# First pair's up products placed beside the last two sequences, and key products of a batch in two row groups

## What is computed

```python
x = x + L0_attn(layernorm(x))   # gated delta rule, 8 key heads, 16 value heads, head size 64
x = x + L0_ffn(layernorm(x))    # 8 routed experts (top 2) and a shared one, hidden size 176
x = x + L1_attn(layernorm(x))   # softmax attention, 16 heads of 8, and a gelu MLP
x = x + L1_ffn(layernorm(x))    # 8 routed experts (top 2) and a shared one, hidden size 512
```

```python
S = S * exp(g_t)                          # g_t: log decay of a value head
delta = (v_t - S.T @ k_t) * b_t
S = S + outer(k_t, delta);  o_t = S.T @ q_t
```

## Time and profile before

| what | value |
|---|---|
| median of 3 runs | 1583.46 us (1576.72 to 1585.36) |
| the profiled execution, its own time | 1569.76 us |
| its span, first to last instruction | 1567.9 us |
| mean TensorE clock granted in it | 0.878 of full speed |
| PE busy | 1321.6 us, 84% of the span |
| DVE busy | 911.5 us |
| ACT busy | 726.7 us |

### The profile page before, as it was taken

The page is one execution under the profiler, slowest core; times in us unless marked ns, Lnnn a source line. Parts: engine busy times, 40 slices in busy tenths (PEclk is TensorE's granted clock), DMA queues, the critical chain, the costliest instruction groups (busy, mean ns, idle before and its releaser), DMA issues.

```text
span 1567.9 us, 26862 instructions
## 1 busy us (share of the span) xinstructions
PE 1321.6 (84%) x11048; PEld 956.3 (61%) x11048; DVE 911.5 (58%) x2365; ACT 726.7 (46%) x1353; POOL 194.2 (12%) x186
## 2 busy tenths in 40 slices
PE   2759889798979979887859786989899988989899
PEld 2345767566666756656846453676566655676567
DVE  4696878979697897968134623463344524354321
ACT  1547465664746566472414143523444344533442
POOL 5011121212122121212020001000000001000000
PEclk9768869798896978887679777999999999999999
DMA  3000000000000000000210000000000000000000
GB/s 120 4 1 4 1 2 11 2 11 2 11 1 2 11 2 8 2 30 2 84 75 1 8 1 0 0 8 1 1 8 1 8 1 7 1 1 1 2 7 8
DMA packets 15066, 17.69 MB, mean 11 GB/s; under 512 B 2567, under 2 KB 13216, under 8 KB 14560
## 3 DMA queue, kind: packets, MB, share of 16 engines
q1 hardware_dynamic: 12768, 14.09, 2.7%
q0 software_dynamic: 576, 1.76, 0.3%
q10 hardware_dynamic: 1600, 0.12, 0.1%
HBM read 13.87 MB, written 2.10 MB: 10 GB/s over the span
## 4 chain that ended last, share of the span: by engine, by line
PE 60%; DVE 25%; ACT 9%; issue 3%; POOL 1%; DMA 1%; SPq 0%; DVEq 0%; ACTq 0%
PE ps L1405 8%; PE ps L1395 8%; PE ps L1354 6%; PE ps L1036 5%; DVE arena L1746 4%; DVE arena L1749 4%; PE ps L1018 4%; DVE arena L1990 2%; ACT arena L900 2%; PE ps L1497 2%; PE ps L1094 2%; PE ps L1461 2%; PE ps L1074 2%; PE ps L1003 1%; PE ps L1184 1%
## 5 line engine op out<-in xcount | busy, mean ns | idle before, releaser
L1664 DVE SCALAR_TENSOR_TENSOR arena<-ps,conv_w,arena 128x255 f32<-128x255 f32 (+2 forms) x384 | 163.8, 475 | 19.4 <-ACT arena L609 14.9
L853 ACT ACTIVATE arena<-ps 128x512 f32<-128x512 f32 x144 | 85.2, 597 | 180.7 <-PE ps L1395 180.6
L1405 PEld LDWEIGHTS ps<-arena 128*128 128x128 f32 x1152 | 132.6, 192 | 24.8 <-issue 9.9
L1405 PE MATMUL ps<-arena 128*128 128x128 f32 x1152 | 136.9, 277 | 7.1 <-ACT arena L853 4.1
L1395 PE MATMUL ps<-arena 128*128 128x512 f32 x288 | 134.3, 612 | 0.0
L516 POOL TENSOR_TENSOR rstd<-var_eps,half_power 128x2 f32<-128x2 f32 (+1 forms) x28 | 23.3, 832 | 650.9 <-DVE var_eps L1635 650.9
L1911 DVE SCALAR_TENSOR_TENSOR arena<-ps,gates,arena 128x128 f32<-128x128 f32 x128 | 36.0, 343 | 114.0 <-PE ps L1405 113.7
L1036 PE MATMUL ps<-arena 64*128 64x256 f32 x256 | 82.9, 462 | 16.1 <-ACT arena L618 16.1
L1732 DVE TENSOR_TENSOR arena<-ps,arena 128x512 f32<-128x512 f32 x64 | 44.1, 689 | 81.9 <-PE ps L1036 70.5
L2027 DVE TENSOR_REDUCE arena<-ps 128x8 f32<-128x2048 f32 (+1 forms) x24 | 54.9, 2292 | 62.2 <-PE ps L1461 62.2
L1036 PEld LDWEIGHTS ps<-arena 64*128 64x128 f32 x256 | 52.4, 220 | 62.0 <-DVE arena L1734 24.1
(11 more groups left out here) (246 smaller groups left out, 2904.0 us busy)
## 6 DMA issues: line engine op xcount, KB each, us to landing
arena<-in_routed_up SPq DMA_DIRECT2D x1, 2048.0 KB, 9.6
arena<-in_routed_down SPq DMA_DIRECT2D x1, 2048.0 KB, 15.0
x_ln<-in_x SPq DMA_DIRECT2D x8, 128.0 KB, 2.2
arena<-in_w_mix SPq DMA_DIRECT2D x1, 1024.0 KB, 11.0
x_in<-in_x SPq DMA_DIRECT2D x8, 128.0 KB, 2.4
out_x<-x_res SPq DMA_DIRECT2D x8, 128.0 KB, 1.9
arena<-out_x SPq DMA_DIRECT2D x4, 256.0 KB, 2.7
out_x<-arena SPq DMA_DIRECT2D x4, 256.0 KB, 2.2
```

The source lines that it names most:

```text
L853: act.activation(hid1[half][:, i, :], ps[:, banks[i], :], ACT.Gelu).then_inc(s["mgelu"], 1)
L1405: mm = pe.matmul(ps[:, bank, c * P:(c + 1) * P], hid1[half][:, i, c * P:(c + 1) * P], m_down[:, e, i, :], start=(i == 0), stop=(i == HT1 - 1))
L1664: ins = dve.scalar_tensor_tensor(conv_tile(f, m)[:, sh:SEQ], ps[:, PAIR_BANK[p], j * SEQ:(j + 1) * SEQ - sh], conv_w[:, m, TAPS - 1 - sh:T ...
```

## The change

1. **Key products.** Batch b of a chunk takes heads b and b + 4, on partitions 0 to 63 and 64 to 127, and each writes to a bank of its own (3 and 4 for even batches, 5 and 6 for odd ones). The 16 value heads of a batch's sums, exponentials and products are picked to match (`batch_of`, `batch_rows`). The other users of the banks move: the small results from bank 3 to bank 2, tokens of v from 3 and 4 to 2 and 4, transposed heads of the second chunk from 5 and 6 to 7 and 2. Waits change with them: the first key products wait for all 8 convolutions (for 3 before), `solve` of the first chunk waits for all products of the next sequence, and stands behind `project(f, 0)`.
2. **The first pair.** The first pair is loaded, normed and transposed in iteration 6. Its up tiles 0 to 4 stand in iteration 6, tiles 5 to 12 and the routing in iteration 7, tile 13 behind the last projection, each on PE, ACT and DVE. For this pair two sets of two banks are used (three before) and one product buffer; there are 3 gate buffers (4 before). Later pairs keep the order of before.

```diff
@@ -72,15 +72,22 @@
-PAIR_BANK = (0, 1, 2, 4, 3, 4, 3, 4)
-KK_BANK = (2, 4)
+PAIR_BANK = (0, 1, 3, 4, 2, 4, 2, 4)
+KK_BANKS = ((3, 4), (5, 6))
+HT_BANKS = ((6, 6), (7, 2))
+V_BANKS = (2, 4)
+FIRST_TURN, FIRST_LOGITS = (0, 7), (2, 6)
...
@@ -387,6 +409,11 @@
+                if it == SEQS - 2:
+                    sp.wait_ge(s["o_psum"], 4 * (SEQS - 1))
+                    sp.wait_ge(s["x1_stored"], 16 * 2)
+                    sp.dma_start(pair_in[:, :, :], pair(out, 0)).then_inc(s["pair_loaded"], 16)
                 if has_i:
                     sp.wait_ge(s["x_updated"], CH * (it + 1))
...
-            sp.dma_start(pair_in[:, :, :], pair(out, 0)).then_inc(s["pair_loaded"], 16)
...
+            def gate_of_tile(p, k):
+                act.wait_ge(s["up_psum"], p * UP0 + k + 1)
+                act.activation(gate3[k % 3], ps[:, up_bank(p, k) + 1, :], ACT.Identity, bias=b3[:, UP_ORDER[k]:UP_ORDER[k] + 1])\
+                    .then_inc(s["gate_done"], 1)
...
                 if has_i:
                     squares(i, 0)
+                if it == SEQS - 1:
+                    hidden_tiles_of(0, 5)
+                    gate_of_tile(0, 6)
+                    gate_of_tile(0, 7)
+                    router(0, 0)
+                if has_i:
                     solutions(i, 1)
+                if it == SEQS - 1:
+                    hidden_tiles_of(0, 7)
...
@@ -1024,17 +1100,17 @@
                 if k == 0:
                     pe.wait_ge(s["qk_silu"], QK_TILES * (n + 1))
-                    pe.wait_ge(s["conv_done"], NP * n + 3)
+                    pe.wait_ge(s["conv_done"], NP * (n + 1))
                 elif k == 1:
-                    pe.wait_ge(s["conv_done"], NP * (n + 1))
+                    after(pe, "u64_ready", 4 * n)
...
-                    m, r = khead(2 * b + g)
-                    mm = pe.matmul(ps[:, KK_BANK[k % 2], 2 * P * g:2 * P * (g + 1)].rearrange("p (q n) -> p q n", q=2),
-                                   mix_qk[n % 2][r:r + DH, QK_TILES + m, cs], mix_qk[n % 2][r:r + DH, m::QK_TILES, cs],
+                    r = DH * g
+                    mm = pe.matmul(ps[:, KK_BANKS[k % 2][g], 0:2 * P].rearrange("p (q n) -> p q n", q=2),
+                                   mix_qk[n % 2][r:r + DH, QK_TILES + b, cs], mix_qk[n % 2][r:r + DH, b::QK_TILES, cs],
                                    start=True, stop=True)
...
@@ -1136,9 +1212,8 @@
                     pe.wait_ge(s["u64_ready"], 4 * (i + 1))
                     pe.wait_ge(s["vtok_ready"], 4 * (i + 1))
-                    after(pe, "hzT_ready", 4 * i - 1)
-                if c == 0 and g == 1:
-                    after(pe, "hzT_ready", 4 * i)
+                    if i + 1 < SEQS:
+                        pe.wait_ge(s["pt_ready"], CH * NB * (i + 2))
...
-            def turn_heads(i, n, c, j, has_n):
+            def turn_heads(i, n, c, j, has_n, has_f):
...
                 elif j == 0:
                     pe.wait_ge(s["hz_ready"], 4 * (i + 1))
-                else:
-                    pe.wait_ge(s["x_updated"], CH * i + 1)
+                    if has_n:
+                        pe.wait_ge(s["u64_ready"], 4 * (n + 1))
+                elif has_f:
+                    pe.wait_ge(s["conv_done"], NP * (n + 2))
+                elif has_n:
+                    pe.wait_ge(s["vtok_ready"], 4 * (n + 1))
                 for m in range(4):
                     at_m = 8 * j + 2 * m
-                    mm = pe.transpose(ps[:, (6 if c == 0 else 5 + j), m * P:(m + 1) * P],
+                    mm = pe.transpose(ps[:, HT_BANKS[c][j], m * P:(m + 1) * P],
                                       hz_slot(i, c)[:, at_m:at_m + 2, :].rearrange("p a b -> p (a b)"), ident)
                 mm.then_inc(s["hzT_psum"], 1)
...
+            def turn_first(i):
+                pe.wait_ge(s["h_ready"], i * N_LN + 1)
+                if i == 0:
+                    pe.wait_ge(s["dm_ready"], CH * NB * SEQS)
+                for c in range(G):
+                    mm = pe.transpose(ps[:, FIRST_TURN[i > 0], c * P:(c + 1) * P], h_tok[:, c, :], ident)
+                mm.then_inc(s["hT_psum"], 1)
...
+            def route_first(p):
+                pe.wait_ge(s["w_b_in"], 16 * 10)
+                pe.wait_ge(s["w1_in"], 16)
+                pe.wait_ge(s["hT_ready"], p * N_HT + 1)
+                if p == 0:
+                    pe.wait_ge(s["hzT_ready"], 4 * (SEQS - 1))
+                for c in range(G):
+                    mm = pe.matmul(ps[:, FIRST_LOGITS[p > 0], E * c:E * (c + 1)], hT0[:, c * P:(c + 1) * P], gate_w[:, :],
+                                   start=True, stop=True)
+                mm.then_inc(s["lg_psum"], 1)
...
+            def up_tile(p, k):
+                if p == 0 and k >= 2:
+                    pe.wait_ge(s["prod_ready"], k - 1)
+                elif p > 0 and k >= 3:
...
+                i = UP_ORDER[k]
+                for j, w in enumerate((w1, w3)):
+                    mm = pe.matmul(ps[:, up_bank(p, k) + j, :], w[:, i * P:(i + 1) * P], hT0[:, :], start=True, stop=True)
+                mm.then_inc(s["up_psum"], 1)
...
+                if has_f:
+                    project(f, 0, n, has_n)
                 if has_i:
                     solve(i, 0, 0)
-                if has_f:
-                    project(f, 0, n, has_n)
-                if has_i:
                     solve(i, 0, 1)
...
+                if it == SEQS - 2:
+                    turn_first(0)
...
+                if it == SEQS - 2:
+                    pe.wait_ge(s["w1_in"], 16)
+                    pe.wait_ge(s["w_b_in"], 16 * 10)
+                    pe.wait_ge(s["hT_ready"], 1)
+                    pe.wait_ge(s["pt_ready"], CH * NB * SEQS)
+                    up_tile(0, 0)
...
+                if it == SEQS - 1:
+                    up_tile(0, 10)
+                    up_tile(0, 11)
+                if has_i:
+                    turn_heads(i, n, 1, 0, has_n, has_f)
+                    turn_heads(i, n, 1, 1, has_n, has_f)
+                if it == SEQS - 2:
+                    up_tile(0, 4)
+                if it == SEQS - 1:
+                    up_tile(0, 12)
             project_out(SEQS - 1, SEQS, 1, False)
+            up_tile(0, 13)
...
+                if it > 0:
+                    route_first(it)
+                    for k in range(UP0):
+                        up_tile(it, k)
+                else:
+                    pe.wait_ge(s["x_updated"], CH * SEQS)
                 pe.wait_ge(s["rw_ready"], it * N_RT + 1)
...
-                pe.wait_ge(s["prod_ready"], it * UP0 + UP0 - 2)
+                pe.wait_ge(s["prod_ready"], it * UP0 + (UP0 - 2 if it > 0 else UP0))
...
-                qk = ps[:, KK_BANK[k % 2], :].rearrange("p (k q n) -> p k q n", k=2, q=2)
-                d = dm[n % 2][:, heads, :].rearrange("p (k v) n -> p k v n", k=2)
-                dve.tensor_tensor(at[:, heads, :].rearrange("p (k v) n -> p k v n", k=2),
+                lo, hi = KK_BANKS[k % 2]
+                qk = ps[:, lo:hi + 1, 0:2 * P].rearrange("p g (q n) -> p g q n", q=2)
+                d = batch_rows(dm[n % 2], c, b)
+                dve.tensor_tensor(batch_rows(at, c, b),
                                   qk[:, :, 1:2, :].to_broadcast([P, 2, 2, P]), d, ALU.mult).then_inc(s["at_ready"], 1)
                 dve.tensor_tensor(d, qk[:, :, 0:1, :].to_broadcast([P, 2, 2, P]), d, ALU.mult).then_inc(s["pt_ready"], 1)
...
+                    steps_of_inverse(lanes, n, 18, 22)
+                if has_i:
+                    gated(me, i, 1, 0)
+                    gated(me, i, 1, 1)
+                if it == SEQS - 1:
+                    product_of_tile(0, 8)
...
+                if it == SEQS - 1:
+                    product_of_tile(0, 9)
+                if has_i:
+                    residual(i, 0)
+                if it == SEQS - 1:
+                    product_of_tile(0, 10)
+                    product_of_tile(0, 11)
+                if has_i:
+                    normalise(i, 1)
...
+                if it == SEQS - 1:
+                    product_of_tile(0, 12)
+            residual(SEQS - 1, 1)
+            product_of_tile(0, 13)
```

More of the change, by code:

```diff
@@ L83 @@
 AT_MIX, AT_REST = 11520, 13568
+AT_PAIR = AT_MIX + UP0 * P
 def constants():
@@ L184, in program @@
         arena = sb("arena", [P, ARENA])
-        taken = {1: 0, 2: AT_REST}
+        taken = {1: 0, 2: AT_PAIR}
         def carve(phase, shape, at=None):
@@ L222, in program @@
         w_z = carve(1, [VH * DH])
+        mix_qk = [carve(1, [2 * QK_TILES, SEQ])]
+        mix_v = carve(1, [V_TILES, SEQ])
+        hT3 = carve(1, [3, SEQ])
+        dm = [carve(1, [HEADS, P])]
         w_out = carve(1, [V_TILES, P])
-        mix_qk = [carve(1, [2 * QK_TILES, SEQ]) for _ in range(2)]
-        mix_v = carve(1, [V_TILES, SEQ])
+        mix_qk.append(carve(1, [2 * QK_TILES, SEQ]))
         hz = carve(1, [3, VH, DH])
-        hT3 = carve(1, [3, SEQ])
         exp_in = sb("exp_in", [P, CH, 2 * VH])
@@ L237, in program @@
         pad = sb("pad", [P, 1])
```

(53 more changed lines are left out.)

275 lines of the change are left out of this document (158 added, 117 removed).

## The result

The changed kernel takes **1510.11 us** (median of four runs, 1507.54 to 1512.68), the kernel before 1581.33 beside it (four runs): ratio 0.955, 95% interval 0.9517 to 0.9584, 71 us less. Forecast were 43 us and 1540, with a range of 1519 to 1560. The direction was right; the size was not, and of the mechanism one step failed in part 1 and one term in part 2. The profiled executions differ by less: 1569.76 and 1512.68.

The account below looks back on a forecast made before the run. Neither engine alone bounds the kernel: the chain is 60% PE and 25% DVE, which hand over to each other. Key products 19 us plus first pair 24 make 43; 1583.5 - 43 = 1540 us, range 1519 to 1560.

Parts of the forecast that it names:

- The price of a batch: Key products: one batch falls from 1.06 us to 0.72, or 0.53 with perfect overlap, at full clock.
- The full clock begins at the same moment: Key products stretch: TensorE's full clock comes no sooner, so some of the gain of 1.1 us so far is lost.
- now ACT is the limit: Products of a sequence, near 600 us: ACT has 8.8 us of work without a gap, ending at 606.4 to 606.6.
- 2.4 us per sequence, 19 in all: Key products: DVE's last products end 2.4 us earlier in each of 8 sequences, 19 us; bounds 8 and 42.
- Left behind the residual, 2.8 us: End of stage one: tile 13 with its bias and product remains, 2.8 us, or 4.5 at half clock.
- Iteration 6, 5 us: Tiles 0 to 4 among the inverse's levels delay `solve` by 4 us, 5 with less luck, 12 at half clock.
- Iteration 7, 8 us: Last sequence: routing and tiles 5 to 12 delay the residual by 8 us; bounds 5 and 16.
- The median, 13.7 us over the profiled execution: Whole kernel: the runs' median is 13.7 us above the profiled 1569.76, so 43 us come off 1583.5.
- key products don't gain: Rival: the pair of matmuls doesn't overlap, or ACT and waits take the gain; part 2 alone, 1559 us; chance 0.12.
- the tiles cost nearly what they did: Rival: half clock in iteration 6 (12 us) and at the end (16), part 2 gives 9, 1555 us; chance 0.13.
- no change: Rival: both parts taken back by 3 us waits in each iteration and the half clock; about 1580 us; chance 0.03.
- The one that I gave 0.12: Rival: earlier exponentials, 4 us a sequence, the clock stays up, 32 + 30 us gained, 1521 us; chance 0.12.

## Why the prediction was wrong

**The price of a batch** (0.72, or 0.53 by perfect overlap): 0.63, which is the middle. The Trainium skill, TensorEngine Tiling (Array Packing), Theoretical Speedup, gives up to 2x for a dimension of at most 64; the runs agree for the matmuls (0.86 to 0.43) and not for the batch, which keeps its 0.20. I had scaled that part down too. The drain that its Key Properties speak of needs no more than this 0.20, which the batch had before as well.

**The start** (first key products behind the last convolution, 0.3 us lost; two batches in about 2.0): as walked, 0.14 and 2.08 us.

**"The full clock begins at the same moment", and so "now ACT is the limit"**: this failed. I let the turned heads' copies end "at 597.6 there", 9.0 us behind the last convolution (588.62), only 1.0 us earlier than before, since I held the moment of the full clock fixed. In the changed trace they end at 576.60, 7.3 us behind the last convolution (569.27). Sums 2 took 1.74 us, not 2.25, and key products 2 took 0.63, not 1.0, as the clock was up sooner: this sequence has 3.3 us at half clock in the stretch from the last convolution to the last products, and the one that I walked 6.8. ACT's 8.8 us of work are what I counted (576.48 to 585.37), but they begin with the turned heads, which PE delivers; so ACT moved with PE and did not become the limit. The last products on DVE end 17.71 us behind the last convolution (569.27 to 586.98). By my walk it was 19.6, before it was 22.06.

**2.4 us per sequence, 19 in all**: the mean of this stretch over eight sequences was 22.1 us and is 18.3; 8 x 3.8 = 30 us, as the 30.7 to 31.2 measured. At equal half clock the gain is near my 2.4: 20.42 to 17.7 us where some 3.3 us are at half clock, and 22.05 to 19.93 where 6.8 are. What I put at nothing is less half clock. In four traces without the row groups the stretch holds 7.4, 8.4, 8.8 and 8.2 us of it on average and lasts 22.1, 22.6, 23.1 and 22.8; in three with them it holds 5.0, 5.0 and 4.9 and lasts 18.3, 18.3 and 18.2. Why the clock rises sooner no run tested apart. The bounds, 8 to 42, held the 30.

**Waits and banks cost nothing**: right (the kernel with them alone, 1.0021).

**Left behind the residual, 2.8 us**: 3.3, from the projection's end to the down products.

**Iteration 6, 5 us**: 3.8. From the first of the 32 level solves to the first `solve` it was 20.49 us (751.89 to 772.38) and is 24.27 (722.78 to 747.05), of which 1.07 is a pause of PE that the profile doesn't explain. In the changed kernel's second trace it is 22.94 (719.24 to 742.18). The clock rose after tile 0, not after tiles 0 and 1: tile 0 took 3.10 us, the next 1.91.

**Iteration 7, 8 us**: 7.3 against the profile that I had (36.05 us from the first `solve` to the end of the last projection, now 43.36), but 0.8 against the other trace of the same kernel, 42.53 (773.54 to 816.07). So this term was right for one execution and some 7 us too dear for another, and the cause is the clock in the second `solve` and `outputs`. It was right against the one profile by luck: that was the only one of five without early tiles or added matmuls in which `outputs` kept the high clock.

**The median, 13.7 us over the profiled execution, as a constant**: this failed too. I treated the difference as something that both kernels carry alike. Part of it, 6.5 us, lies in the last sequence: there the clock fell behind an idle stretch of PE in four other traces without the early pair, and not in the one I read; the change fills that stretch. The changed kernel's profiled execution lies 2.6 us above its median.

The sum by measured terms: keys 30, pair 40.8 - 3.3 - 3.8 - 0.8 = 32.9 against the second trace of the kernel before, together 63. The two executions that it is taken from, 1577.61 and 1512.68 us, differ by 64.9; the medians differ by 71. For the pair alone there are traces at 1582.48 us (banks alone) and 1540.90 (pair alone). The first of the two begins its down products 42.0 us later: 37.6 come from the last sequence (first `solve` to down products 82.8 and 45.2 us), -1.3 from iteration 6 behind the level solves, and 5.6 lie ahead of those, where PE has the same instructions in both kernels. So the pair is worth some 36 us where it acts, and what these 5.6 us are stays open.

One bound was wrong by its own terms: for part 2, 40.1 - 2.8 - 4 - 5 gives 28, not 31.

Of the rivals, "key products don't gain" falls with the 30.7 us of the keys alone, "the tiles cost nearly what they did" and "no change" with the 39.7 of the pair alone, and "slower" with the waits at 1.0021. The one that I gave 0.12, more than the forecast in both parts, is what came, and further than its 1521. Its mechanism fits too: exponentials earlier, 4 us a sequence, the clock up.

Of what the profile was to show, the two matmuls that start together, the pieces of a batch (0.63) and the 42 to 45 us from the first `solve` to the residual (43.36) are there. An iteration was to be 2 us shorter and is 4.2: seven iterations on, the level solves begin at 722.78 in place of 751.89. The down products begin 3.3 us behind the projection and not 4 to 6.

## What to carry over

When an engine gets faster on a chain, move everything that it feeds by the same amount before calling another engine the limit; a start time read from the old trace is not a bound, and neither is the moment at which the clock rises there. Before needed work is costed into a gap, ask what the gap costs now: an idle TensorE with a burst behind it may pay for the gap twice. And one profiled execution is one draw; where a stretch sits at the edge of the two clock levels, a second profile of the kernel before is worth more than another decimal.

## What was not expected of the hardware

- The same program runs a stretch at either clock: the second `solve` took 3.79 us in one execution and 6.24 in another, though PE was busy 1.9 and 1.8 of the 4 us ahead in them.
- 18 added matmuls, 12.8 us of PE work (six times 2.13), left the time of the kernel before unchanged (0.9985, interval 0.9964 to 1.0006).
- Matmuls with 64 rows on the two halves of the array and on two banks overlap completely: a further pair adds 0.43 us, half of the 0.86 on the same rows.
- More time at the high clock need not shorten a kernel: 282 us at half clock in place of 347 and 326, and no gain.
